# Writing the base of a residual sum early and adding a graph layer's rows by an accumulating scatter

## What is computed

```python
for i in range(n_layers):            # 3
    mu = jnp.mean(x, axis=0)
    var = jnp.var(x, axis=0)
    x = (x - mu) * jax.lax.rsqrt(var + EPS) * gamma[i] + beta[i]
    h = x * src_norm
    agg = jax.ops.segment_sum(h[src], dst, num_segments=N) * dst_norm
    x = jax.nn.relu(agg @ W[i] + b[i])
```

```python
x = x + _L0_gnn_ref(_layernorm(x, axis=-1), ...)
x = x + _L0_ffn_ref(_layernorm(x, axis=-1)[None], ...)[0]
```

## Time and profile before

| | |
|---|---|
| median of 3 runs | 3785.86 us (3785.84 to 3785.95) |
| profiled execution | 3788.61 us, its span 3786.9 us |
| mean granted TensorE clock | 0.898 |
| PE busy | 3244.4 us (86%) |
| DVE busy | 2435.9 us (64%) |
| ACT busy | 1369.5 us (36%) |
| POOL busy | 1242.0 us (33%) |
| moved by DMA | 449.66 MB, 119 GB/s on average |

### The profile page before, as it was taken

The page is one execution under the profiler, slowest core; times in us unless marked ns, Lnnn a source line. Parts: engine busy times, 40 slices in busy tenths (PEclk is TensorE's granted clock), DMA queues, the critical chain, the costliest instruction groups (busy, mean ns, idle before and its releaser), DMA issues. The chain is left out here.

```text
span 3786.9 us, 61965 instructions
## 1 busy us (share of the span) xinstructions
PE 3244.4 (86%) x18244; PEld 2741.1 (72%) x18245; DVE 2435.9 (64%) x6053; ACT 1369.5 (36%) x2564; POOL 1242.0 (33%) x1606
## 2 busy tenths in 40 slices
PE   5855889997775329999999999999969995969999
PEld 1213667776775319999999999999858884847676
DVE  7865877644776764555455455545368886957776
ACT  4632655422111424445444444444311111124443
POOL 4763532222553012223222322232233320035552
PEclk9977999998555559999999999999989997989999
DMA  4305323334996033444444444453321111156663
GB/s 157 102 20 131 107 90 124 99 124 144 316 308 210 6 80 99 135 140 113 127 108 141 108 127 125 126 135 104 79 78 55 56 55 53 72 124 162 156 155 99
DMA packets 256000, 449.66 MB, mean 119 GB/s; under 512 B 70818, under 2 KB 76307, under 8 KB 255367
## 3 DMA queue, kind: packets, MB, share of 16 engines
q1 hardware_dynamic: 182065, 280.74, 22.4%
q0 software_dynamic: 62368, 145.38, 17.6%
q10 hardware_dynamic: 11318, 20.54, 1.4%
HBM read 319.46 MB, written 126.83 MB: 118 GB/s over the span
## 5 line engine op out<-in xcount | busy, mean ns | idle before, releaser
L1519 PE MATMUL experts_psU<-experts_x_hi,experts_up_hi 128*128 128x312 f32 (+1 forms) x1408 | 442.9, 315 | 21.1 <-issue 14.9
L1548 PE MATMUL experts_psY<-experts_hid_hi,experts_dn_hi 128*128 128x312 f32 (+1 forms) x1408 | 438.8, 312 | 0.0
L1520 PE MATMUL experts_psU<-experts_x_lo,experts_up_hi 128*128 128x312 f32 (+1 forms) x1408 | 436.5, 310 | 0.0
L1521 PE MATMUL experts_psU<-experts_x_hi,experts_up_lo 128*128 128x312 f32 (+1 forms) x1408 | 435.9, 310 | 0.0
L1549 PE MATMUL experts_psY<-experts_hid_lo,experts_dn_hi 128*128 128x312 f32 (+1 forms) x1408 | 430.8, 306 | 0.0
L1550 PE MATMUL experts_psY<-experts_hid_hi,experts_dn_lo 128*128 128x312 f32 (+1 forms) x1408 | 429.7, 305 | 0.0
L1478 POOL DMA_INDIRECT experts_xg<-xn,experts_token_i x96 | 129.8, 1352 | 596.9 <-DVE experts_token_i L1656 577.4
L1694 DVE TENSOR_TENSOR experts_hid_lo<-experts_hid,experts_hid_hi 128x312 fp32r<-128x312 f32 (+1 forms) x352 | 161.4, 480 | 252.0 <-ACT experts_hid L1611 252.0
L1609 ACT ACTIVATE experts_hid_hi<-experts_psU,experts_bup 128x312 fp32r<-128x312 f32 (+1 forms) x352 | 183.7, 522 | 320.5 <-PE experts_psU L1521 319.1
L1519 PEld LDWEIGHTS experts_psU<-experts_x_hi,experts_up_hi 128*128 128x128 f32 (+1 forms) x1408 | 265.3, 188 | 22.6 <-issue 20.5
L1686 DVE TENSOR_TENSOR experts_dn_lo<-experts_dn_raw,experts_dn_hi 128x1536 fp32r<-128x1536 f32 (+1 forms) x128 | 207.9, 1624 | 100.4 <-ACT experts_dn_hi L1587 100.3
(11 more groups left out here) (469 smaller groups left out, 8051.2 us busy)
## 6 DMA issues: line engine op xcount, KB each, us to landing
experts_dn_raw<-in_L_ffn_W_down SPq DMA_DIRECT2D x96, 768.0 KB
conv<-gcn_diff SPq DMA_DIRECT2D x120, 256.0 KB, 2.9
all_stage<-in_L_ffn_W_up SPq DMA_DIRECT2D x32, 682.5 KB, 6.9
index_xt<-in_x SPq DMA_DIRECT2D x78, 256.0 KB, 2.8
route_xt<-in_x SPq DMA_DIRECT2D x78, 256.0 KB, 4.6
x<-route_xt SPq DMA_DIRECT2D x78, 256.0 KB, 4.5
xn<-route_xn ACTq DMA_DIRECT2D x78, 256.0 KB, 4.7
two_xt<-x SPq DMA_DIRECT2D x78, 256.0 KB, 2.8
```

Of the source, the lines that this page charges most:

```text
L1519: pe.matmul(acc, up_hi[:, c, cols], x_hi[:, c, :], start=(c == 0), stop=False)
L1520: pe.matmul(acc, up_hi[:, c, cols], x_lo[:, c, :], start=False, stop=False)
L1521: mm = pe.matmul(acc, up_lo[:, c, cols], x_hi[:, c, :], start=False, stop=(c == C - 1))
L1548: pe.matmul(acc, dn_hi[0:w, m, cols], hid_hi[0:w, m, :], start=(m == 0), stop=False)
```

## The change

Layer 1 (base) gets a second job. It computes rest_bias, the relu of layer 2's bias, and writes x + rest_bias to g.x for all nodes: SP loads x in 40 pieces of PX = 125 partitions with RX = 2 rows each (load_x), POOL adds the bias (add_x, eight tiles behind), and SP stores the piece (store_x). g.x gets 128 spare rows after the 10000, with rest_bias in them.

Layer 2 (last) subtracts the bias as the other layers do. Its rows are not stored to conv; POOL adds them to g.x with an accumulating indirect DMA (add_rows, also eight tiles behind), the head of each destination into the node's row and every other edge into the spare row of its partition. Each such scatter waits until the one before has landed. The index, head_row, is computed in gcn_tables.

route loads g.x, which is then the finished sum. Its gather from conv, the addition on DVE and the store of g.x go.

```diff
 def gcn_tables(...):
+            step(v.tensor_scalar(spare_row[:, :], g.pidx[:, :], float(g.N), None, ALU.add))
+            step(v.tensor_scalar(into[:, :], g.edgeD[:, :, 0], spare_row[:, :], None, ALU.subtract))
+            step(v.tensor_tensor(into[:, :], into[:, :], g.head[:, :], ALU.mult))
+            step(v.tensor_scalar(into[:, :], into[:, :], spare_row[:, :], None, ALU.add))
+            v.tensor_copy(g.head_row[:, :], into[:, :])
...
 def gcn_layer(...), SP:
+            def load_x(s, j):
+                landed(sp, x_out, s, j, R, 1)
+                sp.dma_start(xs[0:PX, j, :, :], x.rearrange("(p r) d -> p r d", p=PX)[:, bass.ds(s * RX, RX), :])\
+                    .then_inc(x_in[j], 16)
+
+            def store_x(s, j):
+                at_least(sp, x_added, s, 0)
+                sp.dma_start(g.x[0:N, :].rearrange("(p r) d -> p r d", p=PX)[:, bass.ds(s * RX, RX), :],
+                             xs[0:PX, j, :, :]).then_inc(x_out[j], 16)
+            if base:
+                sp.wait_ge(bias_ready, 1)
+                sp.dma_start(g.x[N:N + P, :], rest_bias[:, :]).then_inc(zero_stored, 16)
+            if not last:
+                tiles(sp, ET, ([(2, store_x), (0, load_x)] if base else []) + [(0, store)], R)
...
 POOL:
+            def add_x(s, j):
+                if isinstance(s, int) and s == 0:
+                    pool.wait_ge(bias_ready, 1)
+                landed(pool, x_in, s, j, R)
+                pool.tensor_tensor(xs[0:PX, j, :, :], xs[0:PX, j, :, :],
+                                   rest_bias[0:PX, :].unsqueeze(1).to_broadcast([PX, RX, D]), ALU.add).then_inc(x_added, 1)
+
+            def add_rows(s, j):
+                landed(pool, stored, s, j, R, 1)
+                pool.tensor_copy(into[:, j, :], g.head_row[:, bass.ds(tile(s), 1)]).then_inc(into_staged, 1)
+                at_least(pool, into_staged, s, 0)
+                at_least(pool, differed, s, 0)
+                landed(pool, stored, s - 1, (j - 1) % R, R)
+                pool.sem_inc(waited, 1)
+                pool.indirect_dma_start(g.x, bass.IndirectOffsetOnAxis(ap=into[:, j, :], axis=0),
+                                        diff[:, j, :], None, compute_op=ALU.add).then_inc(stored[j], 16)
-            tiles(pool, ET, ([(3, root)] if first else []) + [(0, ahead)], R)
+            tiles(pool, ET, ([(8, add_x)] if base else []) + ([(8, add_rows)] if last else [])
+                  + ([(3, root)] if first else []) + [(0, ahead)], R)
...
 DVE, differ:
-                if last:
-                    v.tensor_scalar(diff[:, j, :], psZ[:, j % 2, :], 0.0, None, ALU.max).then_inc(differed, 1)
-                else:
+                if not last:
                     at_least(v, squared, s, R)
-                    v.scalar_tensor_tensor(diff[:, j, :], psZ[:, j % 2, :], 0.0, bias, ALU.max, ALU.subtract)\
-                        .then_inc(differed, 1)
+                v.scalar_tensor_tensor(diff[:, j, :], psZ[:, j % 2, :], 0.0, bias, ALU.max, ALU.subtract)\
+                    .then_inc(differed, 1)
...
 def route(...), SP:
-                sp.sem_inc(waited, 1)
-                landed(sp, stored, t, j, R, 1)
-                sp.dma_start(xt[0:r, j, :], x[bass.ds(t * P, r), :]).then_inc(loaded[j], 16)
-
-            def store(t, j):
-                r = node_rows(g, t)
-                at_least(sp, mixed, t, 0)
-                sp.dma_start(g.x[bass.ds(t * P, r), :], xt[0:r, j, :]).then_inc(stored[j], 16)
-            tiles(sp, NT, [(0, load), (2, store)], R)
+                sp.dma_start(xt[0:r, j, :], g.x[bass.ds(t * P, r), :]).then_inc(loaded[j], 16)
+            tiles(sp, NT, [(0, load)], R)
...
 route, POOL (gather removed) and DVE:
-                v.tensor_tensor(xt[:, j, :], xt[:, j, :], gt[:, j, :], ALU.add).then_inc(mixed, 1)
```

More of the change, by code:

```diff
@@ L559, in gcn_tables @@
         nextkey = ph.sb("nextkey", [ET, 1])
+        spare_row = ph.sb("spare_row", [P, 1])
+        into = ph.sb("into", [P, ET])
         link = ph.sb("link", [ET, P], F32R)
@@ L700, in node_rows, with gcn_layer @@
     return g.N - (g.NT - 1) * P if isinstance(t, int) and t == g.NT - 1 else P
-def gcn_layer(nc, g, layer, source, place, first, total, square, last, rows):
+def gcn_layer(nc, g, layer, source, place, first, total, square, last, rows, x):
     D, ET, N, R = g.D, g.ET, g.N, 4
@@ L713, in gcn_layer @@
     L = 2 if first else 0
+    base = layer == 1
+    PX = 125
+    RX = N // PX // ET
+    assert PX * RX * ET == N
     with Phase(nc, f"gcn{layer}") as ph:
@@ L740, in gcn_layer @@
         dsq = ph.sb("dsq", [P, R, D])
+        if base:
+            rest_bias = ph.sb("rest_bias", [P, D])
+            xs = ph.sb("xs", [P, R, RX, D])
+            x_in, x_out = ph.sems("x_in", R), ph.sems("x_out", R)
+            bias_ready, x_added = ph.sem("bias_ready"), ph.sem("x_added")
+        if last:
+            into = ph.sb("into", [P, R, 1], I32)
+            into_staged = ph.sem("into_staged")
         psS = ph.ps("psS", [P, 512])
@@ L759, in _ @@
         def _(sp):
-            sp.wait_ge(zeroed, 1)
-            sp.dma_start(rows[g.ZERO:g.ZERO + 1, :], bias[0:1, :] if last else zero[:, :]).then_inc(zero_stored, 16)
+            if not last:
+                sp.wait_ge(zeroed, 1)
+                sp.dma_start(rows[g.ZERO:g.ZERO + 1, :], zero[:, :]).then_inc(zero_stored, 16)
             sp.wait_ge(vparts, 1)
@@ L767, in store @@
                 sp.dma_start(rows[bass.ds(tile(s) * P, P), :], diff[:, j, :]).then_inc(stored[j], 16)
[L768 to L771, removed]
+            def load_x(s, j):
[6 more added lines that the diff above has]
+                             xs[0:PX, j, :, :]).then_inc(x_out[j], 16)
+            if base:
+                sp.wait_ge(bias_ready, 1)
+                sp.dma_start(g.x[N:N + P, :], rest_bias[:, :]).then_inc(zero_stored, 16)
+            if not last:
+                tiles(sp, ET, ([(2, store_x), (0, load_x)] if base else []) + [(0, store)], R)
+                for j in range(R):
+                    sp.wait_ge(stored[j], 16 * (ET // R))
+                sp.wait_ge(zero_stored, 32 if base else 16)
+            if base:
+                for j in range(R):
+                    sp.wait_ge(x_out[j], 16 * (ET // R))
         @block.gpsimd
         def _(pool):
+            def add_x(s, j):
[13 more added lines that the diff above has]
+                                        diff[:, j, :], None, compute_op=ALU.add).then_inc(stored[j], 16)
             def gather(s, j):
@@ L801, in ahead @@
                     gather(s, j)
-            tiles(pool, ET, ([(3, root)] if first else []) + [(0, ahead)], R)
+            tiles(pool, ET, ([(8, add_x)] if base else []) + ([(8, add_rows)] if last else [])
+                  + ([(3, root)] if first else []) + [(0, ahead)], R)
+            if last:
+                for j in range(R):
+                    pool.wait_ge(stored[j], 16 * (ET // R))
         @block.tensor
@@ L895, in _ @@
             step(v.memset(zero[:, :], 0.0))
-            if not last:
-                v.sem_inc(zeroed, 1)
+            v.sem_inc(zeroed, 1)
             v.memset(vb[:, :].bitcast(F32), 0.0).then_inc(cleared, 1)
@@ L905, in _ @@
             step(v.tensor_scalar(bias, bias, 0.0, None, ALU.max))
-            if last:
-                v.sem_inc(zeroed, 1)
+            if base:
+                v.tensor_scalar(rest_bias[:, :], g.gcn_bias[:, layer + 1, :], 0.0, None, ALU.max).then_inc(bias_ready, 1)
             def moment_chain():
@@ L1002, in route @@
         psR = ph.ps("psR", [P, 2, 512])
-        loaded, gathered, stored, nstored = (ph.sems(n, R) for n in ("loaded", "gathered", "stored", "nstored"))
-        weights, staged, mixed, stat_step, rooted, normed, turned, copied, routed, taken, waited = (
-            ph.sem(n) for n in ("weights", "staged", "mixed", "stat_step", "rooted", "normed", "turned", "copied",
+        loaded, nstored = ph.sems("loaded", R), ph.sems("nstored", R)
+        weights, stat_step, rooted, normed, turned, copied, routed, taken, waited = (
+            ph.sem(n) for n in ("weights", "stat_step", "rooted", "normed", "turned", "copied",
                                 "routed", "taken", "waited"))
@@ L1044, in root @@
                 pool.tensor_tensor(rstd[:, j:j + 1], mv[:, j, 2:3], g.minus_half[:, 0:1], ALU.pow).then_inc(rooted, 1)
-            tiles(pool, NT, [(0, gather), (2, root)], R)
+            tiles(pool, NT, [(0, root)], R)
             pool.wait_ge(soft, 5)
@@ L1090, in mix @@
                 landed(v, loaded, t, j, R)
-                landed(v, gathered, t, j, R)
                 at_least(v, rooted, t, R)
-                v.tensor_tensor(xt[:, j, :], xt[:, j, :], gt[:, j, :], ALU.add).then_inc(mixed, 1)
-                at_least(v, mixed, t, 0)
                 chain.at(t)
@@ L2494, in program @@
     g.attn = scratch("attn", [g.EP + 1, g.D])
-    g.conv = [scratch(f"conv{n}", [g.EP + 1, g.D]) for n in range(3)]
-    g.x = scratch("x1", [g.N, g.D])
```

(2 more changed lines are left out.)

19 lines of the change are left out of this document (4 added, 15 removed).

## The result

| | before | after |
|---|---|---|
| median, us | 3785.85 | 3990.35 |
| lowest and highest, us | 3784.35, 3785.95 | 3988.8, 3996.57 |
| profiled execution, us | 3788.6 | 3988.8 |
| its span, us | 3786.9 | 3987.1 |
| ratio to before | | 1.0537 [1.0524, 1.0549] |

The change makes the kernel slower by 204.5 us. The forecast was 4028 us with a range of 3935 to 4150: the sign and the range held, and the size was 38 us too large.

What follows compares the result with a forecast made beforehand. Before the change, TensorE was taken to bound the main loops of layers 1 and 2, and transfers to hold routing. Terms: 0 + 236 + 71 - 65 = +242 us; 3788.6 + 242 - 2.75 = 4028 us, range 3935 to 4150.

Steps and rivals of the forecast that it cites:

- Layer 1 on five engines: Layer 1: each load and store of x uses five DMA engines, 10.0 us a tile, +236 us (bounds +196 and +292).
- layer 2 on the chain: Layer 2: each scatter waits for the one before to land, 5.9 us a tile, +71 us (bounds +31 and +127).
- routing on PE: Routing: with half the transfers gone PE sets 2.55 us a tile, -65 us (bounds -75 and -55).
- The tables: Table building: five added VectorE operations are hidden by a DMA wait, 0 us; without it, 1.5 us.
- A: Layer 1: the 125 rows spread over all 16 engines, 5.2 us a tile, +44 us, 3836 us in all; chance 0.08.
- B: Layers 1 and 2: 16 engines and neither layer slowed, keeping routing's whole gain, 3721 us; chance 0.05.
- C: Routing: TensorE gets its full clock, VectorE sets 2.0 us a tile, 43 us less, 3985 us; chance 0.10.
- D: Layer 2: PE's waits let its clock fall, up to 8.2 us a tile, up to another 92 us, 4120 us; chance 0.07.
- The share near 0.31 plus little at 150 to 160 GB/s: Layer 1: sign expected in the DMA share if x uses five engines; over 0.6 would be wrong.
- 10 us between tiles: Layer 1: sign expected, 10 us from one difference to the next.
- scatters 5.9 us apart: Layer 2: sign expected, each scatter beginning soon after the landing before; less than 4.5 us apart would be wrong.
- 2.55 us a tile at 0.5 of the clock: Routing: sign expected, with PE without waits.

Runs made afterwards that it cites:

- free scatters: The changed kernel with four sets of spare rows, so layer 2's scatters no longer wait for the one before: 3939.36 us, 1.0406.
- half of the product: The changed kernel with two of the four feature blocks of the router's product left out: 3959.89 us, 1.0464.
- the four-engine window: Window of layer 1 in the changed kernel with x moved in pieces of 124 partitions instead of 125: 4061.26 us, 1.0729.
- the add shared out: Fastest version: changed kernel with 128-partition pieces of x, scatters not waiting, layer 1's bias added by GpSimd (even tiles) and VectorE (odd): 3751.41 us, 0.9909.

## Why the prediction was right

**The order of the limits.** Layer 1 on five engines, layer 2 on the chain, routing on PE: all three were named, and each fell when its limit was moved (120 and 128 partitions, free scatters, half of the product). The tables cost nothing that can be seen: layer 1's first load of x is issued at 559.1 us, where I had put it at about 558.

**Layer 1: 10.0 us forecast, 9.2 measured, +236 against +205.** This is the term that was mis-sized: 31 of the 38 us. The 237.6 KB per engine and tile are right. The rate was not: 237.6/9.2 = 25.8 GB/s, where I took 23.7. I had read that from transfers with one row of 2 KB per packet and put the 26.3 GB/s of the load with long rows down as the upper bound, both from the earlier trace rows. The packets of x are of 4 KB, and their rate lies close to that bound; the four-engine window gives 26.5. That the length of the packets is the reason is argued from these rows only: no run changed it with the engines kept. GpSimd's add took 2.35 us, 2.1 forecast.

The Trainium skill (DMA: Bandwidth & Descriptors, section "Why a DMA increments its semaphore by 16 and not by 1") gives the count of engines as the largest divisor up to 16. The runs agree at four places: shares of 0.26 and 0.31 for 124 and 125 partitions, 0.94 and 0.96 for 120 and 128. Which engines they are no run shows.

**Layer 2: 5.9 forecast, 5.78 measured, +71 against +65 up to the last landing.** From there to routing's first instruction lie 4 us more than before (5.5 against 1.6), which the sum didn't have. Nearly right by the sum, though its terms were wrong in opposite directions. I took 5.1 + 0.4 us to the landing and 0.4 from there to the next scatter; it was 4.8 and 1.0. The experts' 104 rows took longer to land than these 128, perhaps for the traffic beside them, so adding time for 24 more rows was wrong. And the 0.3 us of the earlier trace rows lies between two issues without a wait: it is no price for a wait. The nearer row was the one that I had as the upper bound, 0.8 us behind the copied index.

**Routing: 2.55 forecast, 2.54 measured, -65 against -65.** The 6.6 us gained at the end of its phase were in no term.

**The rivals.** A (sixteen engines, 3836 us) was wrong about 125 partitions. The kernel with 128 shows what it would have been: 3808.5. Its price was near: 4.75 us a tile in layer 1 where it said 5.2, though the DMA engines that it blamed were not the bound. B (faster, 3721) is the same with no slowing at all. It needed a scatter chain under 4.1 us and fast transfers, and even the best version stays 30 us above it. C (full clock in routing) fell: PE is busy for 10 of 10 us at 0.50, and over 184 of 190. D (clock falling in layer 2) happened a little: 0.92 on average, with the tile on the chain of scatters all the same.

So the Trainium skill's rule (TensorE: Matmul & The Clock Gate, section "The HAM clock gate"), by which a continuously busy engine gets the full clock, doesn't hold for this stage, and the measurement decides. Why routing keeps the low level even when PE has no gap isn't settled here. In layer 1 it was the waits: without them the clock is 1.00. In routing hardly any are left: PE waits 5.7 of 190 us for the normalized rows.

**What was said to show it.** The share near 0.31 plus little at 150 to 160 GB/s: 0.31 alone, 0.44 and 161 GB/s with the rest. 10 us between tiles: 9.2. PE waits for the gather as named. SP's waits go by the view to GpSimd's add (224.6 us), which itself waits for the load of x. In layer 2, scatters 5.9 us apart: 5.78. In routing, 2.55 us a tile at 0.5 of the clock: 2.54.

## What to carry to other kernels

Count the engines that a transfer can be spread over before its bytes: 125 partitions cost 165 us more than 120, and 124 more than either. An average DMA share of 0.44 can hide five full engines; look for a plateau in short windows. When work is moved to an idle GpSimd, price it on VectorE too, and look at what is queued behind every wait that it brings. An accumulating scatter is cheap when each one in flight has its own spare rows, and costs its whole landing time when it has not.

## What the runs showed of the hardware that I had not expected

- A VectorE operation with two inputs in SBUF that starts while GpSimd's add runs ends only after it: 0.69 us becomes 2.18 us on average with pieces of 128 partitions, while the 34 operations there with one input in PSUM (L1017) that start during an add keep their 0.68. It goes the other way as well. With the add shared out, VectorE's own add of two SBUF inputs runs from 650.40 to 651.62, and a gather's issue on GpSimd that starts within it takes 1.75 us instead of 0.99. All 11 issues of layer 1 that start during such an add take longer, 1.1 to 1.9 us, and the other 22 take 1.0:

```profile
650.72 1.75 POOL L850 DMA_INDIRECT gcn_xt<-conv,gcn_idx  x1 [0.81 <-POOL gcn_idx L847]
```

- VectorE adds 128x1024 elements in 1.22 us, GpSimd in 2.37 (medians with the add shared out).
- From the landing of one scatter to the start of the next, which waits for it, lie 0.9 to 1.0 us.
- With x in pieces of 128 partitions the DMA engines moved 362 GB/s at a share of 0.99 beside a fully busy PE.
